# Eight-layer float32 block on one Trainium2 core: keys and values of four heads made ahead of their stage, and a last stage with three pairs of PSUM banks and a 4:4 split of one-hot rows

## The reference, cut to what matters

```python
# stage 1: mixture of 8 experts, top 2, F = 176, with a shared expert (untouched itself)
# stage 2: attention over ctx, H, HD = 16, 128, keys and values come from ctx alone
q = (inputs_q @ Wq).reshape(b, sq, H, HD) * (1.0 / np.sqrt(HD))
k = (inputs_kv @ Wk).reshape(b, skv, H, HD)
v = (inputs_kv @ Wv).reshape(b, skv, H, HD)
attn = softmax(einsum('bqhd,bkhd->bhqk', q, k))
x = x + einsum('bhqk,bkhd->bqhd', attn, v).reshape(b, sq, H * HD) @ Wo
# stage 7: product-key experts plus a gated MLP, HIDDEN 256, INTER 1024, 512 experts, top 8
scores, pk = top_k(all pair sums of the two sides' top 8, 8)
ew = silu(einsum('nh,nkh->nk', x, down_embed[indices])) * softmax(scores)
x = x + silu(x @ gate_w) * (x @ up_w) @ down_w + einsum('nk,nkh->nh', ew, up_embed[indices])
```

## Time and profile before

| | |
|---|---|
| median of three runs | 1333.31 us (1331.17 to 1334.44) |
| the profiled execution: its own time | 1332.05 us |
| the profiled execution: span, first to last instruction | 1330.2 us |
| TensorE busy | 1086.9 us (82%) |
| VectorE busy | 622.7 us (47%) |
| ScalarE busy | 365.7 us (27%) |
| GpSimd busy | 224.2 us (17%) |
| mean granted TensorE clock | 0.909 of full speed |
| DMA moved | 65.31 MB, 49 GB/s |

### The profile page before, as it was taken

One profiled execution on the slowest core, in us unless ns is written; L12 is line 12 of the kernel. 1 busy time (PEld: TensorE's weight loads), 2 busy tenths in 40 slices (PEclk: granted clock), 3 DMA queues, 4 the chain that ended last, 5 costly groups with the idle time before them and its releaser, 6 DMA issues.

```text
span 1330.2 us, 17690 instructions
## 1 busy us (share of the span) xinstructions
PE 1086.9 (82%) x6754; PEld 758.2 (57%) x6754; DVE 622.7 (47%) x1459; ACT 365.7 (27%) x666; POOL 224.2 (17%) x301
## 2 busy tenths in 40 slices
PE   5869895398998889965675499999819999969988
PEld 4655684166667666654564467777605555533466
DVE  6967222434343343357545512222146677438454
ACT  4632121122221222211110112222102444425653
POOL 4313332400000000001111111110071222011232
PEclk9977998599999999998886699999957999979998
DMA  9001132101010010064001511211050000010000
GB/s 264 4 1 64 44 90 78 36 24 33 4 33 33 28 33 4 33 232 159 0 1 44 201 29 33 80 33 28 21 180 15 2 1 1 1 64 0 0 12 20
DMA packets 36954, 65.31 MB, mean 49 GB/s; under 512 B 4456, under 2 KB 27848, under 8 KB 35464
## 3 DMA queue, kind: packets, MB, share of 16 engines
q1 hardware_dynamic: 26504, 47.91, 10.7%
q0 software_dynamic: 3744, 10.23, 2.9%
q10 hardware_dynamic: 6624, 6.03, 1.3%
HBM read 53.93 MB, written 10.22 MB: 48 GB/s over the span
## 4 chain that ended last, share of the span: by engine, by line
PE 70%; DVE 18%; issue 4%; ACT 3%; DMA 3%; POOL 2%; SPq 0%; DVEq 0%; ACTq 0%
PE bank L344 22%; PE bank L1132 11%; PE bank L1156 6%; PE bank L1923 5%; PE bank L1378 4%; PE bank L1386 2%; PE bank L1967 2%; PE bank L1946 2%; PE bank L1938 2%; PE bank L1145 1%; DVE big L1243 1%; PE bank L1363 1%; PE bank L1356 1%; PE bank L1978 1%; PE bank L2371 1%
## 5 line engine op out<-in xcount | busy, mean ns | idle before, releaser
L1132 PE MATMUL bank<-big 128*128 x552 | 153.7, 422 | 3.7 <-ACT big L1006 2.4
L344 PE MATMUL bank<-XNT,big 128*128 128x512 f32 x296 | 140.1, 622 | 14.8 <-issue 9.6
L1132 PEld LDWEIGHTS bank<-big 128*128 128x128 f32 x552 | 96.5, 191 | 50.4 <-issue 11.8
L265 POOL TENSOR_TENSOR rstd<-ve,half 128x1 f32<-128x1 f32 x64 | 38.7, 604 | 494.3 <-DVE ve L259 494.2
L1923 PE MATMUL bank<-big,xs 32*128 32x512 f32 x256 | 85.7, 718 | 37.4 <-DVE xs L271 33.6
L1831 DVE TENSOR_REDUCE big<-bank 128x2 f32<-128x512 f32 x128 | 82.2, 685 | 49.3 <-PE bank L1923 49.2
L344 PEld LDWEIGHTS bank<-XNT,big 128*128 128x128 f32 x296 | 56.4, 198 | 80.3 <-issue 70.7
L1156 PE MATMUL bank<-big 128*128 (+1 forms) x368 | 87.2, 380 | 1.1 <-ACT big L1021 1.1
L1883 ACT ACTIVATE big<-bank 128x1024 f32<-128x1024 f32 x64 | 62.0, 1021 | 67.7 <-PE bank L1946 67.7
L950 DVE TENSOR_TENSOR big<-big,bank 128x704 f32<-128x704 f32 x23 | 20.5, 889 | 124.6 <-ACT big L1014 124.6
L344 PE MATMUL bank<-CTXT,big 128*128 128x512 f32 (+1 forms) x192 | 67.0, 494 | 10.8 <-DMA big<-wvT 10.8
(11 more groups left out here) (340 smaller groups left out, 1878.6 us busy)
## 6 DMA issues: line engine op xcount, KB each, us to landing
big<-m_gu SPq DMA_DIRECT2D x8, 1408.0 KB
big<-a_qkv SPq DMA_DIRECT2D x16, 384.0 KB, 3.9
big<-m_d SPq DMA_DIRECT2D x8, 768.0 KB
yg<-big ACTq DMA_DIRECT2D x46, 128.0 KB, 1.7
big<-m_gu SPq DMA_DIRECT2D x8, 352.0 KB
big<-a_o SPq DMA_DIRECT2D x16, 128.0 KB, 2.4
big<-p_gu SPq DMA_DIRECT2D x1, 2048.0 KB, 7.7
big<-m_d SPq DMA_DIRECT2D x8, 176.0 KB
```

The costliest lines, as they stand in the source:

```text
L265: e.tensor_tensor(k.rstd[p][:, :], k.ve[p][:, :], k.half[:, :], ALU.pow).then_inc(k.ln_rstd, 1)
L344: ins = e.matmul(out, a, b, start=start and n == 0, stop=stop and n == len(pairs) - 1)
L1132: ins = e.matmul(out, xgT[s % 2][:, kb, :], WB[:, bass.ds(at[s] + (kb * 2 * F + c * chunk), chunk)], start=kb == 0, stop=kb == KB - 1)
```

## The change

In stage 2, keys and values of heads 0 to 3 are made in two new functions that run on TensorE and ScalarE before these engines wait for stage 1's X. They go through three pairs of banks (2,3), (4,5), (6,7), into four buffers of keys and four of values in a part of SBUF that stage 1 has left. Weights have four buffers, and SP's order of loads is new. For the heads 0 to 3 only queries are projected in the stage. The layer norm of the stage goes tile by tile and no longer by pairs.

In stage 7, `gate_up` and `embed` use three pairs of banks (0,1), (2,3), (6,7) and three silu buffers; ScalarE makes four one-hot rows of a tile and VectorE four; all `embed` come before the first `down`, and the orders written out by hand change on TensorE, ScalarE and VectorE.

```diff
@@ attention_wide
+    FIRST = 4
-    w3 = [W.take(3, KB, HD) for _ in (0, 1)]
+    w3 = [a.take(3, KB, HD) for a in (W, W, W2, W2)]
-    kT = [A.take(T) for _ in (0, 1)]
-    v = [A.take(NT, HD) for _ in (0, 1)]
+    A = Arena(k.big[:, 8000:16200], 8200)
+    kT = [A.take(T) for _ in range(FIRST)]
+    v = [A.take(NT, HD) for _ in range(FIRST)]
+    def qk_at(h):
+        return 4 * h - 2 * min(h, FIRST)
     def sp(e):
...
+        for h in range(FIRST):
+            load(h)
+        load_o(0)
+        load_o(1)
+        for h in range(H):
+            if h + FIRST < H:
+                if h < FIRST:
+                    e.wait_ge(S["qk_ps"], qk_at(h + 1))
+                else:
+                    e.wait_ge(S["v_ps"], h - FIRST + 1)
+                load(h + FIRST)
+            if 1 <= h < H - 1:
+                e.wait_ge(S["wo_ps"], 4 * h)
+                load_o(h + 1)
     def dve(e):
...
-        ln_tiles_dve(e, k, ch, at0)
+        for t in (0, 1):
+            ln_stats_dve(e, k, ch, t, t)
+        for t in range(NT):
+            ln_norm_dve(e, k, at0 + t, t, t % 2).then_inc(k.ln_out, 1)
+            if t + 2 < NT:
+                ln_stats_dve(e, k, ch, t + 2, t % 2)
+    def act_first(e):
+        for h in range(FIRST):
+            e.wait_ge(S["f_ps"], 2 * h + 1)
+            e.copy(v[h], k.bank[:, first_bank(2 * h):first_bank(2 * h) + 2, :].rearrange("p b (t d) -> p (b t) d", d=HD))\
+                .then_inc(S["f_sb"], 1)
+            e.wait_ge(S["f_ps"], 2 * h + 2)
+            e.copy(kT[h], k.bank[:, first_bank(2 * h + 1):first_bank(2 * h + 1) + 2, :].rearrange("p b n -> p (b n)"))\
+                .then_inc(S["f_sb"], 1)
+    def pe_first(e):
+        for h in range(FIRST):
+            e.wait_ge(wsem[h], 16)
+            for n in (2 * h, 2 * h + 1):
+                if n >= 3:
+                    e.wait_ge(S["f_sb"], n - 2)
+                b = first_bank(n)
+                if n % 2 == 0:
+                    ins = values(e, h, b)
+                else:
+                    for c in (0, 1):
+                        ins = mm(e, k.bank[:, b + c, :], [(w3[h][:, 1, kb], k.CTXT[:, kb, c * HALF:(c + 1) * HALF])
+                                                         for kb in range(KB)])
+                ins.then_inc(S["f_ps"], 1)
     def pe(e):
...
+        e.wait_ge(S["f_sb"], 2 * FIRST)
+        project(0)
+        for h in range(H):
+            scores(h)
+            if h + 1 < H:
+                if h > 0:
+                    e.wait_ge(S["wo_sb"], 4 * h - 2)
+                project(h + 1)
+                if h + 1 >= FIRST:
+                    e.wait_ge(S["v_sb"], h + 2 - FIRST)
             turn_p(h)
+            if h > 0:
+                e.wait_ge(S["qk_sb"], qk_at(min(h + 2, H)) + 2)
+                out_proj(h - 1)
+            pv(h)
@@ peer_mlp
-    MINE = 5
+    MINE, SETS = 4, (0, 2, 6)
...
@@ dve
         def hot_sum(u):
             ob = OB[u % 2]
             ch.wait()
-            e.wait_ge(S["oh"], MINE * (u + 1))
@@ dve, from product(IB + 1) on
+        weighted(0)
         hot_sum(1)
         product(IB + 2)
         hot(2)
         product(IB + 3)
+        weighted(1)
+        hot_sum(2)
         product(IB + 4)
+        hot(3)
         product(IB + 5)
+        weighted(2)
+        hot_sum(3)
         product(IB + 6)
+        hot(4)
         product(IB + 7)
+        hot_sum(4)
+        weighted(3)
+        hot(5)
+        hot_sum(5)
+        weighted(4)
+        hot(6)
...
@@ act, from silu(7) on
-        hot(4, 1)
...
+        hot(4, 2)
+        silu_e(0)
+        silu_e(1)
+        hot(6, 2)
+        silu_e(2)
+        silu_e(3)
+        silu(IB)
+        silu(IB + 1)
+        for n in range(2, IB):
+            silu(IB + n)
+            hot(2 * n + 4, 2)
         for n in range(EB):
+            silu_e(EB + n)
+            if n < 2:
+                hot(20 + 2 * n, 2)
+        for n in range(24, MINE * NT, 2):
+            hot(n, 2)
@@ pe
         def gate_up(n):
...
-            if n >= 2:
-                e.wait_ge(S["h"], n - 1)
+            if n == 2:
+                e.wait_ge(S["r_sb"], 2)
+            if n >= 3:
+                e.wait_ge(S["h"], n - 2)
...
+            if u == 0:
+                e.wait_ge(S["e_sb"], 2 * EB)
...
         for n in range(IB):
             gate_up(IB + n)
+            if n % 2 == 1:
+                turn_w(n // 2)
+        for n in range(EB):
+            embed(EB + n)
+            if n == 2:
+                turn_w(4)
+        for u in range(NT):
             down(u)
             down_e(u)
+            if u in (0, 2, 3):
+                turn_w(5 + (u + 1) // 2)
@@ program, run
             for n, s in enumerate(stages):
+                if who + "_first" in s:
+                    s[who + "_first"](e)
                 if n > 1 and who != "sp":
                     e.wait_ge(k.x_tile, LOADED + 8 * (n - 1))
```

More of the change, by code:

```diff
@@ L1266, in pT_copy @@
                 .then_inc(S["pt_dve"], 1)
[L1268 to L1278, removed]
+        for h in range(H):
+            softmax(h)
+            if h + 1 < H:
+                v_copy(h + 1)
+            pT_copy(h)
+            if h > 0:
+                e.wait_ge(S["wo_sb"], 4 * (h - 1) + 2)
                 out_add(h - 1)
[L1280 to L1283, removed]
         e.wait_ge(S["wo_sb"], 4 * (H - 1) + 2)
@@ L1316, in act @@
         e.sem_inc(S["qk_sb"], 2)
-        qk_copy(0, 0)
[L1318 to L1323, removed]
-        exp(H - 2)
-        qk_copy(H - 1, 1)
-        rest(H - 2, 0)
-        exp(H - 1)
-        rest(H - 1, 1)
+        qk_copy(0)
+        for h in range(H):
+            exp(h)
+            if h + 1 < H:
+                qk_copy(h + 1)
+            rest(h)
@@ new lines, in first_bank, with values @@
+    def first_bank(n):
+        return 2 + 2 * (n % 3)
+    def values(e, h, b):
+        for t in range(NT):
+            ins = mm(e, k.bank[:, b + t // 4, (t % 4) * HD:(t % 4 + 1) * HD],
+                     [(k.CTXT[:, kb, t * P:(t + 1) * P], w3[h % FIRST][:, 2, kb]) for kb in range(KB)])
+        return ins
+    def pe_first(e):
[12 more added lines that the diff above has]
+                ins.then_inc(S["f_ps"], 1)
@@ L1345, in project, with scores @@
                     .then_inc(S["qk_ps"], 1)
-            for t in range(NT):
-                ins = mm(e, bank[:, VB + t // 4, (t % 4) * HD:(t % 4 + 1) * HD],
-                         [(k.CTXT[:, kb, t * P:(t + 1) * P], w3[p][:, 2, kb]) for kb in range(KB)])
-            ins.then_inc(S["v_ps"], 1)
-        def scores(h, p):
-            e.wait_ge(S["qk_sb"], h * 4 + (4 + 2))
+            if h >= FIRST:
+                values(e, h, VB).then_inc(S["v_ps"], 1)
+        def scores(h):
+            e.wait_ge(S["qk_sb"], qk_at(h + 1) + 2)
@@ L1365, in turn_p, with out_proj @@
             ins.then_inc(S["pt_ps"], 1)
-        def out_proj(h, p, half, last=False):
-            e.wait_ge(osem[p], half * 16 + 16)
+        def out_proj(h, last=False):
+            e.wait_ge(osem[h % 2], 16 * (h // 2 + 1))
             e.wait_ge(S["c_sb"], h + 1)
@@ L2039, in peer_mlp @@
     eT = A.take(2, EB, HALF)
-    sg = [A.take(HALF) for _ in (0, 1)]
+    sg = [A.take(HALF) for _ in SETS]
     away = [W.take(NE) for _ in (0, 1)]
```

209 lines of the change are left out of this document (61 added, 148 removed).

## The result

The kernel after takes 1288.44 us (median of four runs, 1285.94 to 1293.75) where the kernel before, timed beside it, takes 1333.30: a ratio of 0.9671 [0.9636, 0.9705], 44.9 us less. The forecast was 1287.5. The profiled execution took 1285.94 us with a span of 1284.1; the working had it at 1286.2.

The account below looks back on a forecast made before the run. TensorE was taken to bound stages 2 and 7. Stage 2's 39.0 us (1.1 + 6.2 + 22.1 + 9.6) plus stage 7's 6.8 made 45.8 us, giving 1287.5 us as median; range 1278 to 1299.

Parts of the forecast that it names:

- the cover's edge: Gap before stage 2: four heads' keys and values (28.4 us) fit to 0.1 us; spill taken as 0, bounds 0 and +3.
- rival 4: Keys and values spill out of the gap at half clock, ending 28.4 us late: 1316 us; 0.06 together with the sixth rival.
- The layer norm: Stage 2's layer norm, done tile by tile, takes 8.4 us in place of 9.5: gain 1.1 us.
- head 0's scores: Stage 2: with only queries to project, scores start at 264.8 and not at 270.99: gain 6.2 us.
- Heads 0 to 2: Stage 2: only queries of the next head remain to project, gaining 7.36 us per head, 22.1 us for three.
- Rival 1: Clock falls in the heads projecting only queries (5.8 us) and half of stage 7's gain is lost: 1297 us; chance 0.10.
- The Trainium skill's rule on transposes: Transposes don't count as busy for the clock as products do; in heads 1 and 2 that would cost 5.8 us.
- SP's order: Stage 2: six "issue" waits are weights loaded late; the new load order removes them, gain 9.6 us, bounds 0 and 9.6.
- Stage 7: New order shortens the last stage by 6.8 us, bounds 0 and 12, with turn waits of about 0.5, 0.9 and 2.2.
- The 1.2 us for a fallen clock: Stage 7: behind the 2.2 us wait the clock may fall, costing up to 2.0 us, of which 1.2 was taken.
- The slower one: TensorE, robbed of its rest between stages 1 and 2, is held at half clock in stage 2: about 1347 us; chance 0.02.
- Rival 6: The work meant for the gap stands behind a wait and starts late, 28.4 us back: 1316 us; 0.06 together with the spill.

Follow-up runs that it names:

- e4: Kernel after with the four heads' keys and values made behind the wait for stage 1's X, outside the gap: 1315.39 us, 0.9858 of before.
- e5: Kernel after with three heads' keys and values made ahead in place of four: 1296.97 us, 0.9718 of before.
- a_again: Kernel after, unchanged, timed once more on the chip of the run with swapped turn_p and context banks: 1293.31 us, 0.9685 of before.
- e9: Kernel after with turned probabilities in banks 4 and 5, pv's result in 2 and 3, and waits moved to match: 1275.52 us, 0.9535 of before.
- e11: Kernel after with stage 7 on two pairs of banks, two silu buffers and the old 5:3 split of one-hot rows, new order kept: 1292.88 us, 0.9669.
- e12: Kernel after with ScalarE making a tile's four one-hot rows in one go in stage 7: 1291.61 us, 0.9672 of before.
- e2: Kernel before with only the new last stage (stage 7): 1325.59 us, 0.9933 of before.
- e3: Kernel before with one edit, SP loading weights and output weights head by head and not pair by pair: 1324.72 us, 0.9924 of before.
- e8: Kernel after with ScalarE's four one-hot rows per tile in one go and product 7 ahead of hot(0) on VectorE: 1290.78 us, 0.9646 of before.
- e1: Kernel after with the last stage's function (stage 7) as it was before: 1295.35 us, 0.9693 of before.
- e6: Kernel before with ScalarE making four of a tile's eight one-hot rows and VectorE four: 1332.35 us, 0.9972 of before.

## Why the prediction was right

**The bound and the cover.** TensorE was the bound of stage 2 and the gap was room on it: e4 costs 28.05 us for the 28.4 predicted (by small terms that cancel, as told at e4), e5 7.15 for 7.1. I took 0 for the cover's edge with bounds of 0 and +3. After shows 0. But four later traces (a_again, e9, e11, e12, all of one chip) show "issue" waits within the third of the four heads, in e11 also in the fourth, as here in a_again:

```profile
240.60 2.02 PE L344 MATMUL bank<-CTXT,big 128*128 128x512 f32 x3 [0.80 <-issue]
243.46 0.59 PE L344 MATMUL bank<-CTXT,big 128*128 128x512 f32 x1 [0.83 <-issue]
244.85 1.86 PE L344 MATMUL bank<-CTXT,big 128*128 128x512 f32 x2 [0.81 <-issue]
...
254.47 0.60 PE L317 MATMUL bank<-ident,xs 128*128 128x128 f32 x4
```

That head takes 246.51 - 234.56 = 12.0 us and not 7.0, and the next 8.0. The waits are 2.8 us of the 5.9 lost; the rest is a slower clock between and behind them (granted: 0.85 from 240 to 247, 0.82 from 246.6 to 251.2). The first transposes come 254.47 - 247.75 = 6.7 us after the memset and not 2.7; the layer norm catches up 1.4 of it, and stage 2 is 2.5 us longer (5.2 in e12, where the first projection is slow too). So rival 4's mechanism, work that spills and runs in part at a lower clock, exists at a tenth of its size, and the edge was rightly not called safe. What TensorE waits for there stays open: the profile names nothing, and no run here takes it apart.

**The layer norm** gained 1.5 us (8.0 between first and last transposes, for 9.5), predicted 1.1; **head 0's scores** come 7.54 us earlier after the memset, predicted 7.3.

**Heads 0 to 2** took 297.85 - 263.69 = 34.16 us for 57.72, a gain of 23.6 against 22.1. The period of heads 1 and 2 was the one that I had worked out (5.75 + 6.52 = 12.27, measured 12.23), though the transposes waited 0.93 to 1.00 where I wrote about 1.5. The 1.4 us that are left over are head 0, which took 9.70 and not the 11.1 of my sum: its context product takes 2.02 us with a wait of 0.88 ahead of it, and before it took 3.47:

```profile
286.07 3.47 PE L1386 MATMUL bank<-big 128*128 128x128 f32 x16 [0.88 <-DVE big L1265]
```

This isn't the change's doing. The granted clock was 0.56 there and 1.00 in after, but e2, with before's stage 2, has 2.02 as well, and e11 and e4, with the new one, have 3.56 and 3.65. The product was slow in 5 of the 14 traces and at full clock in 9, behind the same wait each time. So 1.4 of the 40.9 us are chance. Rival 1's first half fell here: out_proj keeps 3.87 in heads 1 and 2. Its second half fell with stage 7's 7.6. The Trainium skill's rule on transposes ("TensorE: Matmul & The Clock Gate", section "PE-mode transpose"), by which 5.8 us would have been paid, isn't borne out by these rows, though with 0.93 us idle the rule was tried more lightly than I had assumed. Head 0 leaves it open: there idle, transposes and a second wait follow each other (1.00, 1.09 and 0.88 us), and the products behind were slow in 5 of 14 traces.

**SP's order** gave 9.7 alone (e3), for 9.6; in the kernel after, 9.8 are left for it and whatever else is in stage 2.

**Stage 7** gave 7.6 for 6.8. The three waits were named at the right tiles with 0.5, 0.9 and 2.2 us and measured 0.92, 0.61 and 2.64. The 1.2 us for a fallen clock behind the longest was not paid in after: 3.72 for the first down. It was paid in e9, whose 2.65 us wait is followed by 3.46 for the four embed matmuls that take 1.88 in after: from that turn to the first down it needs 4.75 us for after's 3.06. Of the six traces with this stage 7, five kept the clock there. I had split the loss as if it were an average, and it is one or the other. Tile 5's stretched rows (4.51) are hidden, as I said, and so are tile 6's (4.75), which I had not seen: by my schedule only tile 5's were to meet POOL.

The two halves' errors, 1.9 and 0.8 us too little gain, were met by 2.2 us more in the middle, which no part of the change touches. So the last digits of the agreement are luck, and so are the 1.4 us of head 0; the mechanism was right in every term but the 1.2 us for the clock, and the range was not needed.

**The other rivals.** The slower one (TensorE held back in stage 2 for want of rest) doesn't show: 0.99 over 294 us at 91% busy, as at 89% before. Rival 6 doesn't either: the work starts at 218.82, right behind stage 1's last product.

## What to carry to other kernels

Where the profile has "issue" in front of matmuls that read weights, look at what stands ahead of that load in its DMA queue; the cure can be an order. A gap in which the bound engine waits for a gather has room for whatever depends on constants alone: four heads brought 28 us (e4), and the last of them still its full 7.15 (e5). Before waits are shortened, look which buffer they guard: another 17.8 us (e9) lay in which two banks the transposes take. And before a difference of 1 to 3 us between two traces is put down to an edit, see whether the same matmuls ran at the same granted clock: four such differences here (head 0, e11, e8, e12) were that.

## What I had not expected of the hardware

- The clock behind a wait is not a function of its length. 2.78 us in front of the embeds took it away in e8 (0.70 over the 10 us behind) and left it in e5; 2.64 (after) and 2.65 (e9) at the same turn differ in the same way. Before, a turn's wait of 2.13 us (at 1269.01) left it full and the next one of 2.15 (at 1282.16) didn't; in e1, with the same code and the same two waits, it was the other way round. Even 0.88 us behind transposes did it in 5 of 14 traces. In stage 7 only the waits of 3.0 us and more (3.02 in e6, 3.88 in before, e1 and e3) cost something every time. What decides wasn't isolated.
- Four f32 one-hot rows on VectorE take 1.9 us alone and 4.3 to 5.0 beside POOL's sums; the tensor-tensor sums of 1024 and 512 columns stretch too, from 1.21 to 3.10 and from 0.69 to 2.73 (after).
- Executions of one kernel spread by up to 11 us (e9, e4), and between traces the stages that no version here changes differ by up to 6.
